# A graph attention layer in split fp32: the first turned tile's high part and the first half slab's low part change engines

## The chip, the cores and the metric

The kernel runs on one core of one Trainium2 chip. The metric is device time in microseconds (us) of that core, in runs without a profiler; three runs of the kernel before gave 288.67, 288.79 and 288.88 us. The median is 288.79 us.

## What is computed

The reference is one graph attention layer on 384 nodes with 1024 features (N = 384, F = 1024, 16 heads of 64). Cut to what matters:

```python
h = relu(layernorm(x))                       # 384 x 1024
q, k, v = h @ wq.T + bq, h @ wk.T + bk, h @ wv.T + bv
q2, k2, v2 = q @ wiq.T + biq, k @ wik.T + bik, v @ wiv.T + biv
scores = q2 . k2 * 0.125 + mask              # per head, mask from 6528 edges
out = softmax(scores) @ v2                   # per head
return x + out @ wo.T + bo
```

## The kernel before, in words

**Split products.** Every fp32 factor of a matrix product is kept as a high part (the value rounded to the matmul's fp32r form, names ending in `_hi`) and a low part (value minus high part, `_lo`). A product is then three matmuls into one PSUM bank: high by high, weight-low by high, high by feature-low. TensorE's time is almost all such triples, over 56 weight slabs of 128 x 1024 that stream in from memory through three buffers `raw` and are split into four pairs `w_hi`, `w_lo`.

**Who does what.** The order on each engine is written out by hand, one program per engine, and semaphores join them. ScalarE makes the high parts of the slabs, VectorE the low parts of slabs 2 to 52, GpSimd those of slabs 0, 1 and the last ones. SyncE issues slab `s` when slab `s - 3` has its low part (for slab 3 also when `half_lo` is there, line 376).

**The start**, where the change is. The rows of `x` come in three tiles of 128 rows (t = 0, 1, 2).
- VectorE takes each tile's statistics, GpSimd the reciprocal root (`rstd`, line 447), ScalarE scales tiles 0 and 1 (line 591). For the last tile VectorE subtracts and clips (line 806), and the scaling is shared: ScalarE scales columns 0 to 511 in two pieces (line 581), VectorE columns 512 to 1023 (line 810, semaphore `h_last_ok`).
- TensorE turns h so that features lie on partitions: 24 transposes of 128 x 128 (`turn_h`, line 1032), eight for each tile. For the last tile the order of k is 0, then 4 to 7 (after `h_last_ok`), then 1, 2, 3. The eight turned tiles `k` of 128 x 384 stand in PSUM; `h_turned` counts them as they are complete.
- ScalarE splits the first half of slab 0 (line 577, `half_hi`) before its share of the last scaling. Then it copies the eight turned tiles to `a_hi` (line 603, `h_hi`): tile 0 as soon as one is turned, tile 1 when six are turned, that is when k = 1 is, tile 2 when seven are, the rest when all are.
- VectorE, after line 810, makes the low part of the first half of slab 0 (line 812, `half_lo`), the high part of the second half (line 815, `early_hi`), and then the eight low parts `a_lo` of the turned tiles (line 856, `h_lo`), each after its `a_hi`.
- GpSimd, after the last `rstd` (line 447), makes the low part of slab 0's second half (line 470, `slab_lo`), then both halves of slab 1 (lines 455 and 458).
- TensorE's `first_tile` follows the turns: per `k` it multiplies slab 0's high part (line 1072) and low part (line 1075) with `a_hi[k]`, and, two steps behind, slab 0's high part with `a_lo[k]` (line 1062, `low_part`). It waits for `half_hi`, for each `a_hi`, for `half_lo` before the first low product, for `slab_lo` before `k` = 4, and for each `a_lo`. Its 24 matmuls are followed without a gap by the tiles of lines 983 to 985.

Of the kernel before, what the change touches and what calls it, by code (L numbers as in the profile page):

```python
# [12 lines left out]
F32 = mybir.dt.float32  # L13
# [4 lines left out]
ALU = mybir.AluOpType  # L18
# [8 lines left out]
KT = F // P  # L27
# [8 lines left out]
HALF = 512  # L36
# [41 lines left out]
def gat_kernel(nc, slabs, x, edge_cols, edge_rows, edge_weights, biases, bo, out):  # L78
    with ExitStack() as ctx:
        def sb(name, shape, dt):  # L80
            return ctx.enter_context(nc.sbuf_tensor(name, shape, dt))

        def sem(name):
            return ctx.enter_context(nc.semaphore(name))
# [3 lines left out]
        a_hi = sb("a_hi", [P, KT, N], F32R)  # L88
# [6 lines left out]
        raw = sb("raw", [P, RAW, F], F32)  # L95
        w_hi = sb("w_hi", [P, RING, F], F32R)
        w_lo = sb("w_lo", [P, RING, F], F32R)
# [68 lines left out]
        def cell_rows(c):  # L166
# [30 lines left out]
        mask_step, mask_ok = sem("mask_step"), sem("mask_ok")  # L197
        stats_step, stats_agg, eps_ok, rstd_ok, shift_ok, h_ok = (
            sem("stats_step"), sem("stats_agg"), sem("eps_ok"), sem("rstd_ok"), sem("shift_ok"), sem("h_ok"))
        h_step, h_last_ok = sem("h_step"), sem("h_last_ok")  # L200
        h_turned, h_hi, h_lo = sem("h_turned"), sem("h_hi"), sem("h_lo")
        half_hi, half_lo, early_hi, second_lo = sem("half_hi"), sem("half_lo"), sem("early_hi"), sem("second_lo")
        second_hi = sem("second_hi")
# [17 lines left out]
        def h_all(k):  # L221

            return h_bank[k][:, 0:N] if k < KT - 1 else banks[:, 0:NT, N:N + P]

        def as_turned(a, k):

            return a[:, k, :] if k < KT - 1 else a[:, k, :].rearrange("p (t m) -> p t m", m=P)
# [32 lines left out]
        def tile_place(t):  # L260

            if t < KT:
                return b_hi[:, t, :], b_lo[:, t, :], bias[:, BV + t:BV + t + 1], tile_bank[t % 2]
            if t < 3 * KT:
                j = t - KT
                hi, lo = (b_hi, b_lo) if j < KT else (c_hi, c_lo)
                return hi[:, j % KT, :], lo[:, j % KT, :], bias_qk[:, j // 2, j % 2:j % 2 + 1], tile_bank[t % 2]
            pair, x = (t - 3 * KT) // 2, t % 2
            hi, lo, b = [(q2_hi, q2_lo, BIQ), (k2_hi, k2_lo, BIK)][x]
            return hi[:, :], lo[:, :], bias[:, b + pair:b + pair + 1], bank[pair_place(pair) + x]  # L270
# [28 lines left out]
        def split_place(s):  # L299

            j = s - O0 - KS
            if Q0 <= s < QK0:
                first = (s - s % 2) % RING
                return tuple(a[:, first:first + 2, :].rearrange("p a (k x d) -> p a k x d", x=2, d=D)[:, :, :, s % 2, :]
                             for a in (w_hi, w_lo))
            if j < 0:
                return w_hi[:, s % RING, :], w_lo[:, s % RING, :]
            hi, lo = (b_hi, b_lo) if j < 3 else (c_hi, c_lo)
            part = slice(j % 3 * F, (j % 3 + 1) * F)
            return tuple(a[:, :, :].rearrange("p k n -> p (k n)")[:, part] for a in (hi, lo))  # L310
# [24 lines left out]
        def wait_lo(eng, s):  # L335

            eng.wait_ge(slab_lo_dve if lo_by_vector(s) else slab_lo, lo_count(s))
# [24 lines left out]
        def _(sp_eng):  # L362
# [50 lines left out]
            for i, (_, n, cols_out, _) in enumerate(out_pieces):  # L413
                sp_eng.wait_ge(out_ok, i + 1)
                sp_eng.dma_start(out[n * P:(n + 1) * P, cols_out], y[:, n, cols_out]).then_inc(stored, 16)
# [3 lines left out]
        def _(pool):  # L419
# [44 lines left out]
            def pair_lo_part(pair):  # L464
                pool.wait_ge(head_hi, pair + 1)
                nc.gpsimd.tensor_tensor(a_lo[:, pair, :], head_out, a_hi[:, pair, :].bitcast(F32),
                                        ALU.subtract).then_inc(head_lo, 1)

            pool.wait_ge(early_hi, 1)
            nc.gpsimd.tensor_tensor(w_lo[:, 0, HALF:F], raw[:, 0, HALF:F], w_hi[:, 0, HALF:F].bitcast(F32),  # L470
                                    ALU.subtract).then_inc(slab_lo, 1)
# [66 lines left out]
        def _(act):  # L538
# [6 lines left out]
            def tile_hi_part(t):  # L545
                hi, _, b, psum = tile_place(t)
                act.wait_ge(slab_used, slabs_done(t))
                if t == KT:
                    act.wait_ge(bias_ok, 4)
                nc.scalar.activation(hi, psum[:, 0:N], ACT.Identity, bias=b).then_inc(tile_hi, 1)  # L550
# [28 lines left out]
            def scale_last(part):  # L579

                nc.scalar.activation(x_sb[:, NT - 1, part], x_sb[:, NT - 1, part], ACT.Copy,
                                     scale=rstd[:, NT - 1:NT]).then_inc(h_ok, 1)
# [3 lines left out]
            for t in range(NT):  # L586
# [6 lines left out]
                else:  # L593
                    act.wait_ge(h_step, 1)
                    act.wait_ge(rstd_ok, NT)
                    for part in (slice(0, P), slice(P, HALF)):
                        scale_last(part)
            for k in range(KT):
                if k == KT - 1:
                    act.wait_ge(h_lo, NT)  # L600

                act.wait_ge(h_turned, 1 if k == 0 else min(k + 1 + KT // 2, KT))
                nc.scalar.activation(as_turned(a_hi, k), h_all(k), ACT.Copy).then_inc(h_hi, 1)
                if k == KT - 3:
                    act.wait_ge(slab_in[1], 16)
                    nc.scalar.activation(w_hi[:, 1, 0:HALF], raw[:, 1, 0:HALF], ACT.Copy).then_inc(second_hi, 1)
# [109 lines left out]
        def _(dve):  # L716
# [87 lines left out]
            for b in range(2):  # L804
# [3 lines left out]
            dve.wait_ge(rstd_ok, NT)  # L808
            dve.wait_ge(h_step, 2)
            nc.vector.tensor_scalar(h_last, h_last, rstd[:, NT - 1:NT], None, ALU.mult).then_inc(h_last_ok, 1)  # L810
            dve.wait_ge(half_hi, 1)
            nc.vector.tensor_tensor(w_lo[:, 0, 0:HALF], raw[:, 0, 0:HALF], w_hi[:, 0, 0:HALF].bitcast(F32),
                                    ALU.subtract).then_inc(half_lo, 1)
            dve.wait_ge(slab_in[0], 16)
            nc.vector.tensor_copy(w_hi[:, 0, HALF:F], raw[:, 0, HALF:F]).then_inc(early_hi, 1)

# [35 lines left out]
                                               op1=ALU.add).then_inc(mask_ok, 1)  # L852

            for k in range(KT):
                dve.wait_ge(h_hi, k + 1)
                nc.vector.tensor_tensor(as_turned(a_lo, k), h_all(k), as_turned(a_hi, k).bitcast(F32),
                                        ALU.subtract).then_inc(h_lo, 1)
            edge_sign()
# [116 lines left out]
            for i, (_, n, cols_out, psum) in enumerate(out_pieces):  # L975
                dve.wait_ge(out_done, i + 1)
                nc.vector.tensor_tensor(y[:, n, cols_out], psum, y[:, n, cols_out], ALU.add).then_inc(out_ok, 1)

        @block.tensor
        def _(pe):  # L980
# [73 lines left out]
            def first_tile():  # L1054

                hi, lo = split_place(0)
                psum = tile_place(0)[3]

                def low_part(k):

                    pe.wait_ge(h_lo, k + 1)
                    return nc.tensor.matmul(psum[:, 0:N], hi[:, k * P:(k + 1) * P], a_lo[:, k, :], start=False,  # L1062
                                            stop=(k == KT - 1))


                pe.wait_ge(half_hi, 1)
                for k in range(KT):
                    c = slice(k * P, (k + 1) * P)
                    pe.wait_ge(h_hi, k + 1)
                    if k == KT // 2:  # L1070
                        wait_lo(pe, 0)
                    nc.tensor.matmul(psum[:, 0:N], hi[:, c], a_hi[:, k, :], start=(k == 0), stop=False)  # L1072
                    if k == 0:
                        pe.wait_ge(half_lo, 1)
                    nc.tensor.matmul(psum[:, 0:N], lo[:, c], a_hi[:, k, :], start=False, stop=False)  # L1075
                    if k >= 2:
                        low_part(k - 2)
                low_part(KT - 2)
                low_part(KT - 1).then_inc(slab_used, 1)

            first_tile()
            for t in range(KT):
                if t >= 1:
# [218 lines left out]
```

## Time and profile before

| What | Value |
| --- | --- |
| median of three runs | 288.79 us |
| profiled execution, its own time | 289.49 us |
| span of its profile | 287.7 us |
| busy: TensorE, VectorE, ScalarE, GpSimd | 281.7, 177.8, 158.0, 151.6 us |
| granted TensorE clock, mean | 1.0 |

The span runs from the first to the last instruction in the profile; the execution's own time has 1.8 us around it. The profiled execution took 0.70 us more than the median run. A busy time is the sum over an engine's instructions, and says nothing of what waited for what.

### The profile page before, as it was taken

The page shows a single profiled execution, that of the slowest core. Times are in us where ns is not written, and L with a number is a line of the kernel's source. Part 1 is how long each engine was busy: PE and PEld are TensorE (multiplying, and loading weights), DVE is VectorE, ACT ScalarE, POOL GpSimd, SP SyncE. Part 2 cuts the span into 40 slices and gives each one's busy share as a digit, 9 for nine tenths or more (in the row PEclk, how much of TensorE's full clock was granted, in tenths as well). Part 3 has the DMA queues.
Part 4 walks back from the last instruction along what each step waited for, and adds up shares of the span by engine and source line. Part 5 has one row for each costly group of instructions (what it writes and reads, how often), then busy time and mean ns, then how long its engine had stood idle before and what let it go on. Part 6 is the DMA issues. An engine that isn't in the chain of part 4 may idle for free.

```text
span 287.7 us, 6029 instructions
## 1 busy us (share of the span) xinstructions
PE 281.7 (98%) x2361; PEld 266.1 (92%) x2361; DVE 177.8 (62%) x442; ACT 158.0 (55%) x287; POOL 151.6 (53%) x157
## 2 busy tenths in 40 slices
PE   6999999999999999999999999999999999999996
PEld 3899998888899999999999999999999999898885
DVE  4999878777588443335564877666667566754221
ACT  2986444193166434323442697977878787985000
POOL 6451354545345765545102597957658494786100
PEclk9999999999999999999999999999999999999999
DMA  7978955744942334455947323605132231221032
GB/s 261 317 246 267 343 202 170 237 154 134 366 159 79 126 96 143 146 146 119 266 117 179 75 66 84 148 8 142 47 102 75 73 90 62 76 99 49 0 146 75
DMA packets 16080, 40.92 MB, mean 142 GB/s; under 512 B 3738, under 2 KB 5171, under 8 KB 16051
## 3 DMA queue, kind: packets, MB, share of 16 engines
q1 hardware_dynamic: 13602, 38.53, 42.7%
q0 software_dynamic: 2016, 1.21, 1.8%
q10 hardware_dynamic: 432, 0.79, 0.7%
q8 instruction: 19, 0.31, 0.4%
q14 instruction: 11, 0.08, 0.1%
HBM read 37.71 MB, written 2.81 MB: 141 GB/s over the span
## 4 chain that ended last, share of the span: by engine, by line
PE 95%; DVE 2%; issue 1%; ACT 1%; POOL 0%; POOLq 0%; ACTq 0%
PE banks L1110 24%; PE banks L983 17%; PE banks L985 17%; PE banks L984 17%; PE banks L1176 6%; PE banks L1129 4%; PE banks L1158 3%; PE banks L1208 3%; PE banks L1028 2%; DVE v L830 1%; PE banks L1032 1%; PE banks L1072 1%; ACT v L570 1%; PE banks L1075 0%; PE banks L1062 0%
## 5 line engine op out<-in xcount | busy, mean ns | idle before, releaser
L489 POOL DMA_INDIRECT cells<-value,cell x51 | 54.1, 1061 | 53.7 <-DMA cells<-value,cell 37.9
L543 ACT ACTIVATE w_hi<-raw 128x1024 fp32r<-128x1024 f32 x50 | 51.8, 1055 | 23.2 <-PE banks L985 19.1
L983 PE MATMUL banks<-a_hi,w_hi 128*128 128x384 f32 x184 | 61.5, 334 | 0.7 <-DVE b_lo L820 0.7
L985 PE MATMUL banks<-a_lo,w_hi 128*128 128x384 f32 x184 | 61.5, 334 | 0.0
L984 PE MATMUL banks<-a_hi,w_lo 128*128 128x384 f32 x184 | 61.5, 334 | 0.0
L462 POOL TENSOR_TENSOR w_lo<-raw,w_hi 128x1024 fp32r<-128x1024 f32 x15 | 36.7, 2451 | 41.0 <-ACT w_hi L543 41.0
L843 DVE TENSOR_TENSOR w_lo<-raw,w_hi 128x1024 fp32r<-128x1024 f32 x35 | 42.3, 1228 | 10.7 <-ACT w_hi L543 10.7
L983 PEld LDWEIGHTS banks<-a_hi,w_hi 128*128 128x128 f32 x184 | 34.5, 188 | 1.0 <-issue 1.0
L984 PEld LDWEIGHTS banks<-a_hi,w_lo 128*128 128x128 f32 x184 | 34.5, 188 | 0.0
L985 PEld LDWEIGHTS banks<-a_lo,w_hi 128*128 128x128 f32 x184 | 34.5, 188 | 0.0
L655 ACT ACTIVATE prob<-prob,neg_max 128x384 f32<-128x384 f32 x48 | 29.0, 605 | 5.2 <-DVE neg_max L903 5.2
L515 POOL TENSOR_SCALAR prob<-prob,row_inv 128x384 f32<-128x384 f32 x48 | 28.2, 604 | 4.0 <-DVE row_inv L911 3.9
L903 DVE CUSTOM_DVE_ANT_0 prob<-banks,work 128x384 f32<-128x384 f32 x48 | 24.7, 555 | 8.9 <-PE banks L1129 8.6
L917 DVE TENSOR_TENSOR pt_lo<-banks,pt_hi 128x768 fp32r<-128x768 f32 x24 | 21.7, 952 | 9.4 <-ACT pt_hi L666 9.4
L1110 PE MATMUL banks<-b_hi,w_hi 64*128 64x384 f32 x128 | 23.9, 347 | 0.0
L1110 PE MATMUL banks<-c_hi,w_lo 64*128 64x384 f32 x128 | 23.0, 331 | 0.0
L1110 PE MATMUL banks<-c_lo,w_hi 64*128 64x384 f32 x128 | 23.0, 331 | 0.0
L1110 PE MATMUL banks<-c_hi,w_hi 64*128 64x384 f32 x128 | 23.0, 331 | 0.0
L1110 PE MATMUL banks<-b_lo,w_hi 64*128 64x384 f32 x128 | 23.0, 332 | 0.0
L1110 PE MATMUL banks<-b_hi,w_lo 64*128 64x384 f32 x128 | 22.9, 332 | 0.0
L666 ACT ACTIVATE pt_hi<-banks 128x768 fp32r<-128x768 f32 x24 | 17.9, 810 | 2.1 <-PE banks L1158 2.0
L985 PE MATMUL banks<-w_lo,b_hi 128*128 128x512 f32 x48 | 18.7, 389 | 0.0
(152 smaller groups left out, 590.2 us busy)
## 6 DMA issues: line engine op xcount, KB each, us to landing
raw<-in_slabs SPq DMA_DIRECT2D x40, 512.0 KB
raw<-in_slabs SPq DMA_DIRECT2D x32, 256.0 KB
prob<-key_rows SPq DMA_DIRECT2D x8, 256.0 KB, 3.7
x_sb<-in_x SPq DMA_DIRECT2D x3, 512.0 KB
out_y<-x_sb SPq DMA_DIRECT2D x5, 256.0 KB, 2.1
cells<-prob SPq DMA_DIRECT2D x2, 576.0 KB, 8.0
cells<-value,cell POOLq DMA_INDIRECT x51
x_sb<-in_x ACTq DMA_DIRECT2D x3, 256.0 KB, 4.6
```

Source lines behind the costliest of these rows:

```text
L462: nc.gpsimd.tensor_tensor(lo, raw[:, s % RAW, :], hi.bitcast(F32), ALU.subtract).then_inc(slab_lo, 1)
L489: nc.gpsimd.indirect_dma_start(out=cells[c][:, :], out_offset=bass.IndirectOffsetOnAxis(ap=cell[:, t:t + 1], axis=0), in_=value[:, t:t + 1 ...
L515: nc.gpsimd.tensor_scalar(prob_chunk(j, n, x), prob_chunk(j, n, x), row_inv[:, j % 2, c:c + 1], 1.0, ALU.mult, ALU.mult).then_inc(prob_ok, 1)
L543: nc.scalar.activation(split_place(s)[0], raw_place(s), ACT.Copy).then_inc(slab_hi, 1)
L655: nc.scalar.activation(prob_chunk(j, n, x), prob_chunk(j, n, x), ACT.Exp, scale=-1.0, bias=neg_max[:, j % 2, c:c + 1], accum_out=row_sum[: ...
L843: nc.vector.tensor_tensor(lo, raw_place(s), hi.bitcast(F32), ALU.subtract).then_inc(slab_lo_dve, 1)
L903: nc.vector.tensor_tensor_reduce(out=prob_chunk(j, n, x), in0=in_blocks(bank[score_place(n) + x][:, 0:N]), in1=in_blocks(mask[:, n, :]), s ...
L917: nc.vector.tensor_tensor(as_turned_probs(pt_lo, m), turned(pair, m), as_turned_probs(pt_hi, m).bitcast(F32), ALU.subtract).then_inc(pt_lo ...
L983: nc.tensor.matmul(psum, w[0], a[0], start=first, stop=False)
L984: nc.tensor.matmul(psum, w[1], a[0], start=False, stop=False)
L985: return nc.tensor.matmul(psum, w[0], a[1], start=False, stop=last)
L1110: mm = nc.tensor.matmul(bank[pair_place(pair) + x][:, 0:N], w[own, k * P:(k + 1) * P], a[own, block_at % KT, :], start=(step == 0), stop=( ...
```

## The change

VectorE now copies turned tile 0 to `a_hi` (new semaphore `h_first`), at the place where it made the first half slab's low part. GpSimd makes that low part, ahead of its other half slab. ScalarE copies tiles 1 to 7 only. Whoever waited for `h_hi` waits for `h_first` at k = 0 and for a count that is one lower after it. Nothing is added or left out of the computation.

```diff
@@ gpsimd, after the last rstd
+            pool.wait_ge(half_hi, 1)
+            nc.gpsimd.tensor_tensor(w_lo[:, 0, 0:HALF], raw[:, 0, 0:HALF], w_hi[:, 0, 0:HALF].bitcast(F32),
+                                    ALU.subtract).then_inc(half_lo, 1)
             pool.wait_ge(early_hi, 1)
@@ scalar
-            for k in range(KT):
+            for k in range(1, KT):
                 if k == KT - 1:
                     act.wait_ge(h_lo, NT)

-                act.wait_ge(h_turned, 1 if k == 0 else min(k + 1 + KT // 2, KT))
+                act.wait_ge(h_turned, min(k + 1 + KT // 2, KT))
                 nc.scalar.activation(as_turned(a_hi, k), h_all(k), ACT.Copy).then_inc(h_hi, 1)
@@ vector, after line 810
-            dve.wait_ge(half_hi, 1)
-            nc.vector.tensor_tensor(w_lo[:, 0, 0:HALF], raw[:, 0, 0:HALF], w_hi[:, 0, 0:HALF].bitcast(F32),
-                                    ALU.subtract).then_inc(half_lo, 1)
+            dve.wait_ge(h_turned, 1)
+            nc.vector.tensor_copy(as_turned(a_hi, 0), h_all(0)).then_inc(h_first, 1)
@@ vector (the low parts) and tensor (first_tile), the same edit in both
-                dve.wait_ge(h_hi, k + 1)
+                if k == 0:
+                    dve.wait_ge(h_first, 1)
+                else:
+                    dve.wait_ge(h_hi, k)
```

VectorE's order from the scaling of the last tile to the low parts, before (`h_last` is a part of `x_sb`):

```order
L810 TENSOR_SCALAR x_sb<-x_sb,rstd 128x512 [waits h_step,rstd_ok]
L812 TENSOR_TENSOR w_lo<-raw,w_hi 128x512 [waits half_hi]
L815 CAST w_hi<-raw 128x512 [waits slab_in0]
L856 TENSOR_TENSOR a_lo<-banks,a_hi 128x384 [waits h_hi] x8
```

and in the changed kernel, whose lines lie a few further down (813 is 810, 817 is 815, 861 is 856):

```order
L813 TENSOR_SCALAR x_sb<-x_sb,rstd 128x512 [waits h_step,rstd_ok]
L815 CAST a_hi<-banks 128x384 [waits h_turned]
L817 CAST w_hi<-raw 128x512 [waits slab_in0]
L861 TENSOR_TENSOR a_lo<-banks,a_hi 128x384 [waits h_first]
L861 TENSOR_TENSOR a_lo<-banks,a_hi 128x384 [waits h_hi] x7
```

The subtraction over 512 columns is gone, and a copy of 384 columns out of PSUM, which waits for the first turned tile, stands in its place.

GpSimd's order from the last `rstd` on, before:

```order
L447 TENSOR_TENSOR rstd<-mean_var,minus_half 128x1 [waits stats_agg]
L470 TENSOR_TENSOR w_lo<-raw,w_hi 128x512 [waits early_hi]
L455 TENSOR_TENSOR w_lo<-raw,w_hi 128x512 [waits second_hi]
```

and in the changed kernel:

```order
L447 TENSOR_TENSOR rstd<-mean_var,minus_half 128x1 [waits stats_agg]
L470 TENSOR_TENSOR w_lo<-raw,w_hi 128x512 [waits half_hi]
L473 TENSOR_TENSOR w_lo<-raw,w_hi 128x512 [waits early_hi]
L455 TENSOR_TENSOR w_lo<-raw,w_hi 128x512 [waits second_hi]
```

A third half-slab subtraction stands ahead of the two others, right behind the last `rstd`; line 470 is now the first half, line 473 the second.

## Rows read from the trace of the kernel before

**Rows 1.** Page: the chain that ended last, by engine.
```profile
PE 95%; DVE 2%; issue 1%; ACT 1%; POOL 0%; POOLq 0%; ACTq 0%
```
**Rows 2.** Waits of TensorE (engine line waited for: us, times, longest).
```profile
PE banks L983 <- DVE b_lo L820: 0.7, 1, 0.7
```
**Rows 3.** Timeline of TensorE, 10.6 to 12.2 (start us, us, engine, line, operation, count).
```profile
10.60 0.33 PE L1032 MATMUL banks<-ident,x_sb 128*128 128x128 f32 x1
...
11.20 0.38 PE L1032 MATMUL banks<-ident,x_sb 128*128 128x128 f32 x2
...
11.60 0.41 PE L1072 MATMUL banks<-a_hi,w_hi 128*128 128x384 f32 x1
...
12.06 0.44 PE L1072 MATMUL banks<-a_hi,w_hi 128*128 128x384 f32 x1
```
**Rows 4.** Timeline of ScalarE, 9.4 to 12.0.
```profile
9.43 0.62 ACT L577 ACTIVATE w_hi<-raw 128x512 fp32r<-128x512 f32 x1
...
10.97 0.49 ACT L603 ACTIVATE a_hi<-banks 128x384 fp32r<-128x384 f32 x1
...
11.51 0.49 ACT L603 ACTIVATE a_hi<-banks 128x384 fp32r<-128x384 f32 x1
```
**Rows 5.** Timeline of VectorE, 10.1 to 15.5.
```profile
10.12 0.49 DVE L810 TENSOR_SCALAR x_sb<-x_sb,rstd 128x512 f32<-128x512 f32 x1
10.52 0.68 DVE L812 TENSOR_TENSOR w_lo<-raw,w_hi 128x512 fp32r<-128x512 f32 x1
11.12 0.42 DVE L815 CAST w_hi<-raw 128x512 fp32r<-128x512 f32 x1
11.49 3.99 DVE L856 TENSOR_TENSOR a_lo<-banks,a_hi 128x384 fp32r<-128x384 f32 x8
...
12.04 1.95 DVE L856 TENSOR_TENSOR a_lo<-banks,a_hi 128x384 fp32r<-128x384 f32 x4
```
**Rows 6.** Timeline of GpSimd, 9.2 to 12.9.
```profile
9.18 0.87 POOL L447 TENSOR_TENSOR rstd<-mean_var,minus_half 128x1 f32<-128x1 f32 x1 [0.91 <-DVE mean_var L801]
...
11.62 1.30 POOL L470 TENSOR_TENSOR w_lo<-raw,w_hi 128x512 fp32r<-128x512 f32 x1 [1.57 <-DVE w_hi L815]
```
**Rows 7.** Timelines of VectorE and GpSimd, 15.4 to 16.8.
```profile
15.40 0.16 DVE L735 TENSOR_SCALAR sp<-ew 128x4 f32<-128x4 f32 x1
15.41 1.30 POOL L458 TENSOR_TENSOR w_lo<-raw,w_hi 128x512 fp32r<-128x512 f32 x1
15.47 1.26 DVE L736 TENSOR_SCALAR sp<-ew 128x4 f32<-128x4 f32 x1
```
**Rows 8.** Timelines of both at 166, and line 462 (ns min/median/max).
```profile
166.02 1.22 DVE L933 TENSOR_TENSOR x_sb<-x_sb,prob 128x1024 f32<-128x1024 f32 x1
166.43 3.08 POOL L462 TENSOR_TENSOR w_lo<-raw,w_hi 128x1024 fp32r<-128x1024 f32 x1 [0.39 <-ACT w_hi L543]
...
L462 POOL TENSOR_TENSOR w_lo<-raw,w_hi x15: 2396/2402/3081, 156.2 to 252.5; 128x1024 fp32r<-128x1024 f32 x15
```
**Rows 9.** TensorE's weight loads (PEld) in the first tile, and its end.
```profile
11.68 0.19 PEld L1075 LDWEIGHTS banks<-a_hi,w_lo 128*128 128x128 f32 x1
...
13.42 0.19 PEld L1072 LDWEIGHTS banks<-a_hi,w_hi 128*128 128x128 f32 x1
...
15.68 0.19 PEld L1062 LDWEIGHTS banks<-a_lo,w_hi 128*128 128x128 f32 x1
...
16.03 0.33 PE L983 MATMUL banks<-a_hi,w_hi 128*128 128x384 f32 x1
```
**Rows 10.** Downstream: slab 3, the second tile's low part, TensorE's fourth tile; DMA share.
```profile
17.74 1.06 ACT L543 ACTIVATE w_hi<-raw 128x1024 fp32r<-128x1024 f32 x1 [0.22 <-DMA raw<-in_slabs]
...
23.14 0.62 DVE L820 SCALAR_TENSOR_TENSOR b_lo<-banks,bias,b_hi 128x384 fp32r<-128x384 f32 x1
...
24.35 0.33 PE L983 MATMUL banks<-a_hi,w_hi 128*128 128x384 f32 x1
...
14.00:15.00 1.00, 1.00 (x8) 0.99 (x7) 0.99 (x3) 1.00 (x4) 0.87 (x1) 1.00 1.08 406
```

More of the change, by code:

```diff
@@ L199, in gat_kernel @@
             sem("stats_step"), sem("stats_agg"), sem("eps_ok"), sem("rstd_ok"), sem("shift_ok"), sem("h_ok"))
-        h_step, h_last_ok = sem("h_step"), sem("h_last_ok")
+        h_step, h_last_ok, h_first = sem("h_step"), sem("h_last_ok"), sem("h_first")
         h_turned, h_hi, h_lo = sem("h_turned"), sem("h_hi"), sem("h_lo")
@@ L1068, in first_tile @@
                     c = slice(k * P, (k + 1) * P)
-                    pe.wait_ge(h_hi, k + 1)
+                    if k == 0:
+                        pe.wait_ge(h_first, 1)
+                    else:
+                        pe.wait_ge(h_hi, k)
                     if k == KT // 2:
```

## The prediction

> **What bounds the kernel now.** I read the chain that ended last first: TensorE is 95% of it [rows 1], and its list of waits has one entry behind the start, 0.7 us at about 86 us for a low part of VectorE [rows 2]. From the end of the first tile on, TensorE runs almost without a gap, so the change is worth exactly what it does to the moment when TensorE leaves its first tile, 16.03 us [rows 9], unless something further down absorbs or enlarges that. What matters is the stretch from 10.1 to 16.0 us, read engine by engine.
>
> TensorE first [rows 3]. The first transpose of the last tile starts at 10.60, the one of k = 1 at 11.20 (a row of two, 0.11 apart, so its result stands at about 11.48), and the first product of the first tile at 11.60. The next high product comes at 12.06 only; at full pace it would have come two matmuls of 0.17, or 0.35, after the first. That is the hole that one might hope to close. ScalarE explains it [rows 4]: `a_hi[0]` is made from 10.97 to 11.46, `a_hi[1]` from 11.51 to 12.00, and TensorE goes on at 12.06.
>
> But what held `a_hi[1]`? ScalarE starts back-to-back copies 0.1 before the last one ends, which would be 11.36. It started at 11.51, 0.03 after the transpose of k = 1 was done, and by the program it waits for just that (six tiles turned). So ScalarE was waiting for TensorE, not for its own copy of tile 0. **Taking that copy off ScalarE frees 0.37 us of an engine that then waits for the same transpose.** `a_hi[1]` and all behind it stay where they are, if the transposes do.
>
> **The change part by part.**
>
> *ScalarE* loses 0.49 us of work and gains nothing that can be passed on. Zero.
>
> *GpSimd's new half slab.* It needs `half_hi`, which ends at 9.43 + 0.62 = 10.05 [rows 4], and GpSimd itself is free at 9.18 + 0.87 = 10.05 [rows 6]. GpSimd starts 0.08 after another engine's result (line 470 at 11.62, after the cast that ends at 11.54 [rows 5, 6]), so at 10.13. VectorE starts line 810 at 10.12 [rows 5]: the two start within 0.01 us of each other. This matters since they can hold each other up. A VectorE operation on four columns took 1.26 us where its twin took 0.16, and ended at 16.73, right behind the GpSimd subtraction that ran from 15.41 to 16.71 [rows 7]. The other way round, a GpSimd subtraction that started at 166.43, inside a VectorE one, took 3.08 us against a median of 2.40, and ended 2.27 after the VectorE one had (169.51 less 167.24) [rows 8]. Which is held? Whoever starts first goes on; and the twin of 0.16 us started 0.01 *before* GpSimd and was not held, while the one that started 0.06 after was. At 10.12 VectorE is again 0.01 ahead. My forecast is that VectorE goes first.
>
> Then line 810 ends at 10.61 as now, and so do the transposes. GpSimd, held until 10.61, needs the rest: of 2.40 us for 1024 columns and 1.30 for 512 [rows 6, 8], 1.10 go to 512 columns; behind a release 1024 columns took 2.27, so 512 take 1.17. `half_lo` is ready at **11.78**; before it was 10.52 + 0.68 = 11.20 [rows 5]. TensorE loads these weights at 11.68 now [rows 9]; that moves to 11.83 (a load follows its data by 0.05), 0.15 late. The hole before 12.06 has the room: the six products of k = 0, 1, 2 need 1.04 at full pace. About 0.
>
> *VectorE's copy of tile 0.* The first tile is turned at 10.60 + 0.33 = 10.93, so the copy starts at about 10.98. No row shows a VectorE copy out of PSUM. Nearest below is the cast of 512 columns inside SBUF, 0.42; nearest above the subtraction of 384 columns with one operand in PSUM, 0.55 (the row of four spans 1.95, starting every 0.47) [rows 5]. I take 0.55, for the same PSUM operand and width; `a_hi[0]` is then ready at 11.53, not 11.46, and the first product moves by 0.07 at most, or with 0.42 forward by what the last transposes allow, 0.07. Both vanish in the hole before 12.06. The Trainium skill ("VectorE: DVE Perf Modes", on PSUM operands) says that fp32 out of PSUM runs at one column a cycle; by its cost table (120 + 384 cycles at 0.96 GHz, 0.525 us, an estimate) the sum would be 0.02 less.
>
> *The cast that follows* (`early_hi`) would start at 11.45 where it started at 11.12, but GpSimd is at work until 11.78. A cast inside SBUF is of the kind that I count as held: it ends some 0.28 behind the release, at **12.06** against 11.54 now. So the eight low parts begin at 12.01 instead of 11.49. They start every 0.47 us, their source is there in time, and the last ends at 12.01 + 7 x 0.465 + 0.55 = **15.82**, against 15.48 now (two waits for `a_hi` that they had on the way take up 0.2). TensorE loads the weights of its last low product at 15.68 [rows 9], before that is there: the load moves to 15.87, by 0.19. As the load runs 0.17 ahead of its product, part may be made good; between 0.02 and 0.19 I take **+0.10**.
>
> *Slab 0's second half* on GpSimd starts at 12.14 and ends at 13.44, where it ended at 12.92 [rows 6]. TensorE's load for k = 4 stands at 13.42 [rows 9]: 0.07 late, from 0 to 0.07, inside the same delay and not added to it.
>
> *Downstream.* SyncE issues slab 3 with that low part, 0.5 later. Its data stood behind the fill of the mask cells in a saturated queue (DMA share 1.08 from 14 to 15 us), and ScalarE took slab 3 at 17.74. What follows on VectorE ends with the second tile's low part, 23.14 + 0.62 = 23.76, which TensorE needs at 24.35: 0.4 to 0.5 of room [rows 10]. I expect 0 to 0.3 of lateness there and cost it at nothing; with all 0.5 it would be 0.1.
>
> The sum is +0.10 against the profiled execution's 289.49. That one lies 0.70 above the median, but nothing in the sum is proportional to it, so I add it to the median: 288.79 + 0.10 = **288.9 us**. A measurement of this kernel tells 0.2%, or 0.58 us, from no change.
>
> **The rivals.**
>
> *GpSimd first (slower).* If GpSimd has begun when VectorE wants line 810, that line ends about 0.33 behind GpSimd's 10.13 + 1.30 = 11.43, at 11.76, not 10.61. It gives `h_last_ok`, for which the transposes of k = 4 to 7 wait, and those of 1, 2, 3 stand behind them on TensorE: k = 1 moves by 1.15, with it `a_hi[1]` and the whole tile, and nothing is queued elsewhere that makes it good. 288.79 + 1.15 = 289.94 us. It decides at a lead of GpSimd somewhere between 0 and 0.06 us [rows 7], which is a matter of one or two hundredths here. For it speaks how near the tie is; against it that the twin was not held at a lead of 0.01. The Trainium skill ("SBUF — State Buffer", on who interferes with whom) has this as a rule: the two engines share a pair of SBUF ports, the first to start holds it for its whole instruction, and the other blocks fully. By that rule, the traces agree both ways round. Chance 0.17.
>
> *The copy out of PSUM is held as well.* It would wait for 11.78 and end near 12.2; the cast and the low parts follow, the last ending near 16.3, and the tile ends about 0.6 late: 289.4 us. Against it: the low parts of line 856, which read PSUM and one SBUF operand, start every 0.47 and keep that pace beside GpSimd's work from 11.62 to 12.92 [rows 5, 6]. Chance 0.06.
>
> *ScalarE was the brake after all (faster).* If the freed copy brings `a_hi[1]` forward, at most the holes between 11.53 and 12.90 close, some 0.33 us: 288.5 us, which would not be told from no change. Chance 0.05.
>
> *Something further down moves.* The wait of 0.7 us at 86 us [rows 2] could shrink or grow as the transfers before it shift: 288.1 to 289.5. Chance 0.04.
>
> **How the numbers follow.** The forecast has 0.68, between 288.7 and 289.1. With the rivals, faster by over 0.2% needs the last one on its good side: 0.04. Slower by over 0.2%: GpSimd first 0.17, half of the held copy 0.03, the last one's bad side 0.02, so 0.22. Same: 0.74. The range goes from 288.4, for the closing holes, to 290.1, to hold the tie that falls the other way.
>
> **What would show it.** Line 813 near 10.12 with 0.49 us, and GpSimd's line 470 with 1.65 instead of 1.30: VectorE went first. Line 813 with 1.6 us and line 470 with 1.30: it was the rival. The copy (815) near 10.98 with 0.42 to 0.56. The cast (817) stretched to about 0.6. ScalarE's first copy still at 11.51. The first matmul of line 983's group near 16.1. I am wrong in the mechanism if ScalarE's first copy starts before 11.4, or if no operation of either engine is stretched.

## The result

The changed kernel takes **290.18 us** (median of ten runs), the kernel before 288.82 us in the same comparison: a ratio of 1.005, interval 1.004 to 1.006. That is 1.2 to 1.7 us more. I had forecast 288.9 us and no change that can be told; what happened is the rival "GpSimd first", for which I had worked out 289.94 us and given 0.17. My range ended at 290.1 us. In the experiments below two runs were far longer than the others of their kernel (990.55 us with GpSimd in two pieces, 296.23 us with one empty instruction); the ratios leave them out, the medians as recorded do not, and without them these two medians are 289.44 and 288.8 us.

The profiled execution took 290.15 us, its span is 288.4 us. Its chain is led by TensorE less than before [rows 1], with VectorE's scaling of the last tile (line 813) among its lines:

```profile
PE 89%; DMA 5%; DVE 3%; ACT 1%; issue 0%; SPq 0%; DVEq 0%; ACTq 0%
PE banks L1118 24%; PE banks L988 16%; PE banks L989 16%; PE banks L990 16%; PE banks L1184 6%; PE banks L1137 4%; PE banks L1166 3%; PE banks L1216 3%; DMA raw<-in_slabs 2%; DMA x_sb<-in_x 2%; DVE v L832 1%; ACT w_hi L546 1%; PE banks L1080 1%; DVE x_sb L813 1%; ACT v L573 1%; PE banks L1067 0%
```

The waits of TensorE have a new entry, 0.8 us for line 813, and another of 0.5 us for ScalarE's scaling of the second tile: in this execution VectorE waited 0.5 us for the rows of the last tile (at 7.72), in that of before it did not. The entry that answers to [rows 2] is shorter:

```profile
PE banks L1037 <- DVE x_sb L813: 0.8, 1, 0.8
PE banks L1037 <- ACT x_sb L594: 0.5, 1, 0.5
PE banks L988 <- DVE b_lo L822: 0.2, 1, 0.2
```

The timeline of VectorE in the changed kernel (answers to [rows 5]):

```profile
10.35 1.55 DVE L813 TENSOR_SCALAR x_sb<-x_sb,rstd 128x512 f32<-128x512 f32 x1
11.82 0.54 DVE L815 CAST a_hi<-banks 128x384 fp32r<-128x384 f32 x1
12.29 0.41 DVE L817 CAST w_hi<-raw 128x512 fp32r<-128x512 f32 x1
```

and that of GpSimd (answers to [rows 6]):

```profile
9.41 0.87 POOL L447 TENSOR_TENSOR rstd<-mean_var,minus_half 128x1 f32<-128x1 f32 x1 [0.68 <-DVE mean_var L804]
10.35 1.27 POOL L470 TENSOR_TENSOR w_lo<-raw,w_hi 128x512 fp32r<-128x512 f32 x1
```

Both start at 10.35, as near as I had worked out. But the scaling takes 1.55 us instead of 0.49, and ends at 11.90, 0.28 behind GpSimd's subtraction (11.62), which takes its plain time. What waits for the scaling shows on TensorE and ScalarE (answers to [rows 3, 4, 9]):

```profile
11.96 0.33 PE L1037 MATMUL banks<-ident,x_sb 128*128 128x128 f32 x1 [0.80 <-DVE x_sb L813]
...
12.70 0.42 PE L1080 MATMUL banks<-a_hi,w_hi 128*128 128x384 f32 x1
12.96 0.33 PE L1083 MATMUL banks<-a_hi,w_lo 128*128 128x384 f32 x1
13.30 0.44 PE L1080 MATMUL banks<-a_hi,w_hi 128*128 128x384 f32 x1
...
17.29 0.33 PE L988 MATMUL banks<-a_hi,w_hi 128*128 128x384 f32 x1
```

```profile
12.76 0.87 ACT L606 ACTIVATE a_hi<-banks 128x384 fp32r<-128x384 f32 x2 [1.48 <-PE banks L1037]
```

The transposes go on at 11.96, ScalarE's first copy starts at 12.76 behind them, after 1.48 us of idle time, and the second tile's first matmul (line 988, 983 before) comes at 17.29 instead of 16.03.

The profiled executions differ by up to 0.5 us in when the last `rstd` ends (9.98 to 10.47), since the rows of `x` arrive at different times, so I compare from a point that lies behind that: **from the end of the last `rstd` to the second tile's first matmul** it is 16.03 - 10.05 = 5.98 us before, and 17.29 - 10.28 = 7.01 us now. The first tile costs 1.03 us. This length, called the stretch below, is read in the same way from the one profiled execution of every kernel.

### The profile page after: what moved, and what is told of

Read it like the earlier page. It is cut to its first block, busy times and chain, and to the rows that moved or that the text cites. A ratio compares the mean times of both kernels' runs of the same rounds, so it can differ in the third digit from the quotient of the medians.

```text
span 288.4 us, 6029 instructions
## 1 busy us (share of the span) xinstructions
PE 281.7 (98%) x2361; PEld 265.6 (92%) x2361; DVE 178.8 (62%) x442; ACT 157.3 (55%) x286; POOL 153.3 (53%) x158
## 4 chain that ended last, share of the span: by engine, by line
PE 89%; DMA 5%; DVE 3%; ACT 1%; issue 0%; SPq 0%; DVEq 0%; ACTq 0%
PE banks L1118 24%; PE banks L988 16%; PE banks L989 16%; PE banks L990 16%; PE banks L1184 6%; PE banks L1137 4%; PE banks L1166 3%; PE banks L1216 3%; DMA raw<-in_slabs 2%; DMA x_sb<-in_x 2%; DVE v L832 1%; ACT w_hi L546 1%; PE banks L1080 1%; DVE x_sb L813 1%; ACT v L573 1%; PE banks L1067 0%
```

## The experiments

Theory A is the rival's: GpSimd's subtraction, once under way, holds VectorE's scaling, and through `h_last_ok` the transposes. Theory B says that the moved copy costs. All were compared with the kernel before on the same chip, whose median was 288.83 us beside the first four, 288.73 beside the next four and 288.71 beside the last three. The intervals are of the ratio to it. The number of runs per kernel lies between 4 (two waits more) and 12.

| Run | stretch, us | median, us | ratio (interval) |
| --- | --- | --- | --- |
| before | 5.98 | 288.8 | |
| the change | 7.01 | 290.18 | 1.005 (1.004 to 1.006) |
| GpSimd's part alone | 6.99 | 289.90 | 1.0034 (1.0022 to 1.0047) |
| the copy alone | 6.06 | 289.15 | 1.0006 (0.9995 to 1.0017) |
| VectorE's scaling first | 6.25 | 289.21 | 1.0016 (1.0004 to 1.0028) |
| scaling cut 511 + 1 | 7.15 | 290.20 | 1.0049 (1.0031 to 1.0068) |
| GpSimd in two pieces | 6.49 | 289.61 | 1.0031 (1.0018 to 1.0044) |
| scaling with a running sum | 6.23 | 289.06 | 1.0005 (0.9996 to 1.0015) |
| one wait more | 7.05 | 289.76 | 1.0033 (1.0022 to 1.0043) |
| two waits more | 7.04 | 290.05 | 1.0042 (1.0027 to 1.0057) |
| one empty instruction | 6.03 | 288.83 | 1.0006 (0.9997 to 1.0016) |
| two empty instructions | 6.03 | 288.87 | 1.0003 (0.9994 to 1.0012) |
| tile 4 second (from before) | 5.98 | 288.57 | 0.9997 (0.9988 to 1.0006) |

**GpSimd's part alone.** The copy is back on ScalarE, VectorE has neither job (of the edit to the changed kernel only VectorE's lines are shown; ScalarE's loop and the waits are those of before).

```diff
-            dve.wait_ge(h_turned, 1)
-            nc.vector.tensor_copy(as_turned(a_hi, 0), h_all(0)).then_inc(h_first, 1)
```

> Only GpSimd's part of the change: it makes the first half slab's low part, the copy of tile 0 stays on ScalarE, and VectorE has neither. Theory A: the scaling of the last tile is stretched to about 1.55 us as in the changed kernel, k = 1 is turned 1.0 to 1.15 us late, total 289.9 to 290.3 us. Theory B: 288.8 us as before.

Measured 289.90 us. VectorE's scaling in its timeline:

```profile
10.30 1.55 DVE L813 TENSOR_SCALAR x_sb<-x_sb,rstd 128x512 f32<-128x512 f32 x1
```

The stretch is 6.99 us: the whole loss comes with GpSimd's part, none of it needs the copy. Theory B falls.

**The copy alone.** GpSimd is as before, VectorE keeps its subtraction and copies tile 0 behind it (shown against the kernel before, VectorE's lines only).

```diff
             dve.wait_ge(half_hi, 1)
             nc.vector.tensor_tensor(w_lo[:, 0, 0:HALF], ...).then_inc(half_lo, 1)
+            dve.wait_ge(h_turned, 1)
+            nc.vector.tensor_copy(as_turned(a_hi, 0), h_all(0)).then_inc(h_first, 1)
```

> Only the copy of tile 0 is moved to VectorE, behind the half slab's low part, which stays there. Theory A: the scaling takes 0.49 us, the copy 0.54 us, ScalarE's first copy still starts at the transpose of k = 1, that is where its second one started before; the low parts end 0.3 us later and the tile 0 to 0.2 us: 288.9 us (288.8 to 289.1). Theory B: 290 us or more.

Measured 289.15 us, not told from before by its interval; the stretch is 0.08 longer. ScalarE's first copy starts 1.46 us after the last `rstd` ended (11.94 and 10.47), as its second one did before (11.51 and 10.05). So freeing ScalarE brought nothing forward.

**VectorE's scaling first.**

```diff
+            pool.wait_ge(h_last_ok, 1)
             pool.wait_ge(half_hi, 1)
             nc.gpsimd.tensor_tensor(w_lo[:, 0, 0:HALF], ...)
```

> The changed kernel, but GpSimd takes up the first half slab's low part only after VectorE has scaled the last tile (it waits for h_last_ok). Theory A (GpSimd's subtraction, once begun, holds VectorE's scaling of the last tile and with it the transposes): the scaling is back at 0.49 us and starts and ends first, GpSimd's subtraction follows it from 0.08 behind its end and takes 1.3 us, the cast of early_hi is held until that ends; the tile ends 0.3 us late, total 289.1 us (288.9 to 289.3). Theory B (the copy of tile 0 on VectorE is what costs): nothing comes back, 290.1 to 290.4 us.

Measured 289.21 us. The timelines of VectorE and GpSimd in this run:

```profile
10.27 0.49 DVE L814 TENSOR_SCALAR x_sb<-x_sb,rstd 128x512 f32<-128x512 f32 x1
...
11.12 0.56 DVE L816 CAST a_hi<-banks 128x384 fp32r<-128x384 f32 x1 [0.36 <-PE banks L1038]
11.60 0.80 DVE L818 CAST w_hi<-raw 128x512 fp32r<-128x512 f32 x1
```

```profile
10.84 1.28 POOL L471 TENSOR_TENSOR w_lo<-raw,w_hi 128x512 fp32r<-128x512 f32 x1 [0.64 <-DVE x_sb L814]
```

With nothing but the order at this place changed, 0.76 us of the stretch come back. The copy out of PSUM runs beside GpSimd in 0.56 us; the cast inside SBUF behind it is held until GpSimd is through at 12.12, and takes 0.80. What is left, 0.27, comes in two waits of TensorE:

```profile
12.17 0.19 PEld L1084 LDWEIGHTS banks<-a_hi,w_lo 128*128 128x128 f32 x1 [0.19 <-POOL w_lo L471]
```

```profile
12.48 1.30 POOL L474 TENSOR_TENSOR w_lo<-raw,w_hi 128x512 fp32r<-128x512 f32 x1 [0.36 <-DVE w_hi L818]
```

The first low product waits for the half slab that GpSimd now makes later; behind that TensorE is 0.12 late. The held cast makes slab 0's second half late as well (it ends at 13.78), the load of weights for k = 4 comes 0.12 behind that, at 13.90, and behind it TensorE is 0.26 late. The low parts `a_lo` add 0.01.

**The scaling cut in 511 and 1 columns**, to take it out of the mode in which it handles two columns a cycle.

```diff
-            nc.vector.tensor_scalar(h_last, h_last, rstd[:, NT - 1:NT], None, ALU.mult).then_inc(h_last_ok, 1)
+            for part in (slice(HALF, F - 1), slice(F - 1, F)):
+                piece = x_sb[:, NT - 1, part]
+                nc.vector.tensor_scalar(piece, piece, rstd[:, NT - 1:NT], None, ALU.mult).then_inc(h_last_ok, 1)
```

TensorE waits for both pieces (that line is not shown).

> The changed kernel with VectorE's scaling of 512 columns cut into 511 and 1, odd counts in both. Theory A in its narrow form (only an operation that works at two columns a cycle needs what GpSimd holds): both pieces run beside GpSimd's subtraction, the long one in about 0.69 us instead of 1.56, h_last_ok is 0.27 us late, total 289.1 us (289.0 to 289.4). If any VectorE operation from SBUF to SBUF is held: 290.2 us or more, the pieces ending behind GpSimd's.

Measured 290.20 us.

```profile
10.38 1.55 DVE L815 TENSOR_SCALAR x_sb<-x_sb,rstd 128x511 f32<-128x511 f32 x1
```

It is held, and ends 0.28 behind GpSimd's 11.65, as 512 columns do. The form of the next experiment takes 0.25 us more than the plain one takes unhindered (0.74 and 0.49 us for 512 columns), and no such addition shows behind the release. So I take it that an odd count did not change the mode, and the run tells nothing of what a slower mode would do. That is what the Trainium skill says too ("VectorE: DVE Perf Modes", the mode table: even counts, or equal ones for source and destination); I had overlooked the second half.

**The scaling with a running sum as a second output.** The extra column of sums is read by nothing.

```diff
-            nc.vector.tensor_scalar(h_last, h_last, rstd[:, NT - 1:NT], None, ALU.mult).then_inc(h_last_ok, 1)
+            nc.vector.tensor_scalar(h_last, h_last, rstd[:, NT - 1:NT], 0.0, ALU.mult, ALU.add,
+                                    accum_out=shift[:, NT - 1:NT]).then_inc(h_last_ok, 1)
```

> The changed kernel with VectorE's scaling written with a running sum as a second output (into a column of shift that nothing reads); the sum is not part of the computation. The Trainium skill (SBUF — State Buffer, who interferes with whom) says that this form does not work on two columns a cycle and so does not contend. If so, theory A in its narrow form expects it to run beside GpSimd's subtraction in 0.7 to 0.8 us instead of 1.56, h_last_ok 0.2 to 0.35 us later than before, from the last rstd to the second tile's first matmul 6.2 to 6.4 us, total 289.2 us (289.0 to 289.5). If any VectorE operation from SBUF to SBUF is held by GpSimd's reads: 7.0 us or more, total 290.1 us or more.

Measured 289.06 us, which is not told from before. VectorE and GpSimd in this run:

```profile
10.35 0.74 DVE L813 TENSOR_SCALAR_CACHE_REDUCE x_sb<-x_sb,rstd 128x512 f32<-128x512 f32 x1
```

```profile
10.33 1.27 POOL L470 TENSOR_TENSOR w_lo<-raw,w_hi 128x512 fp32r<-128x512 f32 x1
```

GpSimd started first, by 0.02 us, and nobody was held: VectorE's form ended 0.5 us before GpSimd did, and GpSimd took its plain 1.27. So it is not VectorE as such that GpSimd holds, but this form of its work. The Trainium skill's page "SBUF — State Buffer" (who interferes with whom) names exactly this exception, and the trace agrees.

**GpSimd's subtraction in two pieces** of 256 columns.

```diff
-            nc.gpsimd.tensor_tensor(w_lo[:, 0, 0:HALF], ...).then_inc(half_lo, 1)
+            for part in (slice(0, HALF // 2), slice(HALF // 2, HALF)):
+                nc.gpsimd.tensor_tensor(w_lo[:, 0, part], ...).then_inc(half_lo, 1)
```

(Arguments cut; whoever waits for `half_lo` waits for both pieces.)

> The changed kernel with GpSimd's new subtraction in two instructions of 256 columns. Theory A (VectorE is held for one instruction of GpSimd): the first piece takes about 0.75 us, VectorE's scaling gets in between the two and ends some 0.5 us earlier than in the changed kernel, the second piece waits for it; from the last rstd to the second tile's first matmul 6.4 to 6.6 us (before 5.98, changed 7.01), total 289.4 us (289.2 to 289.8). Theory C (VectorE waits until GpSimd has nothing more ready, since GpSimd takes up its next instruction before the last one ends): the scaling ends later than now, 7.1 us or more, total 290.2 us or more.

Measured 289.61 us.

```profile
10.33 1.01 DVE L814 TENSOR_SCALAR x_sb<-x_sb,rstd 128x512 f32<-128x512 f32 x1
```

```profile
10.33 1.59 POOL L471 TENSOR_TENSOR w_lo<-raw,w_hi 128x256 fp32r<-128x256 f32 x2
```

VectorE got in between the two, ended at 11.34 instead of 11.90, and the second piece waited for it. The hold of VectorE lasts for one instruction of GpSimd; half an instruction, half the loss (the stretch is 0.51 longer than before, not 1.03).

**How much lead does VectorE need?** Four runs delay GpSimd's start by a little. First by more waits, on semaphores that have long come:

```diff
             pool.wait_ge(half_hi, 1)
+            pool.wait_ge(h_step, 2)
```

> The changed kernel with one more wait ahead of GpSimd's new subtraction, on a semaphore that has long come (h_step), which costs GpSimd the handling of one wait, 0.05 to 0.08 us. Theory A with a tie that GpSimd won by less than that: VectorE is now first, the scaling takes 0.49 us, GpSimd's subtraction is stretched to 1.6 us, from the last rstd to the second tile's first matmul 6.05 to 6.25 us, total 288.9 to 289.2 us. If GpSimd claims what they share well before its start in the profile, or is served first whoever comes first: nothing changes, 7.0 us, 290.0 to 290.3 us.

> As the run with one more wait, with two (also stats_agg, long there too): VectorE leads by 0.1 us or more. Theory A: 288.9 to 289.2 us, as with one wait, or, if one was too little, only here. If GpSimd is served first whoever comes first within 0.1 us: 7.0 us, 290.0 to 290.3 us.

Measured 289.76 and 290.05 us. With one wait more:

```profile
10.26 1.59 DVE L814 TENSOR_SCALAR x_sb<-x_sb,rstd 128x512 f32<-128x512 f32 x1
```

```profile
10.30 1.27 POOL L471 TENSOR_TENSOR w_lo<-raw,w_hi 128x512 fp32r<-128x512 f32 x1
```

VectorE leads by 0.04 us and is still held. The second wait added no delay (a lead of 0.03, again held); why not is not shown. Then by an instruction that does nothing:

```diff
             pool.wait_ge(half_hi, 1)
+            nc.gpsimd.engine_nop().then_inc(lead, 1)
+            pool.wait_ge(lead, 1)
```

> The changed kernel with one empty instruction of GpSimd between its wait for half_hi and the new subtraction, passed on by a semaphore of its own: it begins 0.05 to 0.1 us later, so VectorE leads by that. With 0.04 us of lead VectorE lost. If GpSimd's claim counts from within 0.1 us of its start: VectorE is now first, its scaling takes 0.49 us, GpSimd's subtraction 1.6 to 1.7 us; the forecast of the prediction is then tried as it was meant: from the last rstd to the second tile's first matmul 6.05 to 6.25 us (before 5.98, changed 7.01), total 288.9 to 289.1 us. If GpSimd is served first whatever the lead: 7.0 us and 290.0 us.

> The same with two empty instructions, a lead of 0.1 to 0.2 us. If the lead decides, VectorE is first here even if it was not with one: 6.05 to 6.3 us, total 288.9 to 289.2 us. If GpSimd is served first whenever it asks before VectorE is through: 7.0 us or more and 290.0 us.

Measured 288.83 and 288.87 us. The run with one empty instruction:

```profile
10.09 0.49 DVE L816 TENSOR_SCALAR x_sb<-x_sb,rstd 128x512 f32<-128x512 f32 x1
10.94 0.56 DVE L818 CAST a_hi<-banks 128x384 fp32r<-128x384 f32 x1 [0.36 <-PE banks L1040]
11.41 0.58 DVE L820 CAST w_hi<-raw 128x512 fp32r<-128x512 f32 x1
```

```profile
10.16 1.55 POOL L473 TENSOR_TENSOR w_lo<-raw,w_hi 128x512 fp32r<-128x512 f32 x1
```

```profile
16.05 0.34 PE L991 MATMUL banks<-a_hi,w_hi 128*128 128x384 f32 x1
```

A lead of 0.07 us turns it round: the scaling takes 0.49, GpSimd is the one that is held (1.55 instead of 1.27), and the kernel is not told from before. With two empty instructions the lead is 0.14 and the result the same. An instruction that does nothing, ahead of the moved one, takes back the whole loss of the change.

**Tile 4 second.** From the kernel before: is there anything to win in the hole before tile 1?

```diff
+TILE_ORDER = [0, 4, 1, 2, 3, 5, 6, 7]
-            for k in range(KT):
+            for i, k in enumerate(TILE_ORDER):
-                act.wait_ge(h_turned, 1 if k == 0 else min(k + 1 + KT // 2, KT))
+                act.wait_ge(h_turned, (1, 2, 6, 7)[i] if i < 4 else KT)
```

VectorE's low parts and TensorE's products follow the same order, tile 4's high product second (those edits are not shown).

> The kernel before with another order in the first tile: tile 4, turned second, is copied to a_hi second and multiplied second, in the hole in which TensorE waits for tile 1. GpSimd and VectorE keep their work. This asks what closing the hole is worth at most: from the last rstd to the second tile's first matmul 5.80 to 5.90 us instead of 5.98, total 288.5 to 288.8 us, hardly to be told from before (288.8). If the hole is set by something else than the transpose of k = 1: 5.98 us or more.

Measured 288.57 us, not told from before, and a stretch of 5.98: no gain. ScalarE's copies follow each other without a pause; the second to the fourth (tiles 4, 1 and 2):

```profile
11.39 1.25 ACT L607 ACTIVATE a_hi<-banks 128x384 fp32r<-128x384 f32 x3
```

Tile 4's product filled the hole at 12.06, but the copy of tile 1 started at 11.76 instead of 11.51 and ended at 12.25, and its high product came at 12.30. TensorE gained nothing: its eighth product starts at 13.11, 1.48 behind its first, and before it was 13.07, 1.47 behind. The pause of ScalarE that I had found, 0.15 us, was too short for a whole copy; they follow each other every 0.37.

## Why the prediction was wrong

**The step that failed** is the order of the two engines: "the twin of 0.16 us started 0.01 *before* GpSimd and was not held ... At 10.12 VectorE is again 0.01 ahead. My forecast is that VectorE goes first." GpSimd went first, VectorE's scaling took 1.55 us instead of 0.49, and the stretch grew by 1.03. The tie was there, but I read the order of starts wrongly. The twin stood at 15.40 [rows 7], and line 458 of GpSimd followed on line 455 without a pause there: its row begins at 15.41, while line 455, from 14.13 for 1.30 us, was still at work until 15.42. I take it that in such a row GpSimd's own work begins later than the row does, so that the twin was further ahead than 0.01; no run tests this. At 10.12 both engines came out of a wait, and there VectorE's start has to lie further ahead: 0.00, 0.03 and 0.04 us were too little, 0.07 and 0.14 enough. So it is VectorE that needs a lead, between 0.04 and 0.07 us, and not GpSimd, for which I had put 0 to 0.06. No row of before has two such starts, and nothing in the rows spoke for a chance as small as 0.17. By the Trainium skill's rule on the port pair ("SBUF — State Buffer", who interferes with whom) the one that starts first holds it; by the starts that the profile shows, VectorE was 0.04 ahead in one run and lost, so here the measurement decides: the rule does not resolve starts this close.

The other steps, with the run of one empty instruction as the kernel that I had forecast (it is another kernel, and shows what would have followed had VectorE gone first; the forecast of the changed kernel stays wrong):
- *ScalarE's freed time brings nothing.* Right. Where it leaves out tile 0 and VectorE's scaling takes its 0.49 us, its first copy starts 1.46 to 1.47 behind the last `rstd`, as its second one did before; in the changed kernel it comes behind the late transposes.
- *GpSimd held: 1.17 behind the release, `half_lo` at 11.78.* Measured 11.71 less 10.58, 1.14. Right.
- *The copy of tile 0: 0.55, not held beside GpSimd.* Measured 0.56 beside GpSimd, 0.54 in the changed kernel, where GpSimd was through. Right, and the rival that it is held falls.
- *The cast stretched to about 0.6, ending 0.28 behind the release.* Measured 0.58, and 0.28. Right.
- *The tile 0.10 late, 288.9 us.* Measured 0.05, and 288.83 us. The size is near, the place isn't the one I had priced, the last low product. Its load is 0.12 later than before, counted from the last `rstd` (5.75 and 5.63), but the product behind it loses nothing that shows; with two empty instructions it loses 0.02. Of the 0.05, 0.03 appear at k = 4, where TensorE waits for slab 0's second half (through at 13.38 in this run), which I had counted inside the other delay. So it was luck in part that the sum came out.

```profile
13.49 0.19 PEld L1083 LDWEIGHTS banks<-a_hi,w_hi 128*128 128x128 f32 x1
...
15.77 0.19 PEld L1070 LDWEIGHTS banks<-a_lo,w_hi 128*128 128x128 f32 x1
```

- *The rival's price of 1.15.* The stretch is 1.03 longer: the scaling ended 0.28 behind GpSimd, not 0.33, and GpSimd took 1.27, not 1.30. The median rose by 1.36, 0.3 more than the stretch.

**What stays open** is that 0.3. Runs with the same stretch differ as much: 289.76 and 290.05 us with more waits, 289.90 with GpSimd's part alone. A place where the start's lateness can grow or be absorbed is the wait near 87 us [rows 2]: TensorE waits there for a low part of VectorE (line 822), and the chain goes back from it over VectorE and ScalarE to a slab's transfer. In the changed kernel that transfer is the longest piece of the chain between 70 and 90 us:

```profile
73.53 7.11 DMA raw<-in_slabs
...
87.00 0.63 DVE b_lo L822
```

The wait was 0.7 us in the profiled execution of before, 0.2 in the changed one, 0.3 with two waits more, and under 0.1 in the ten others. It accounts for most of what the profiled executions differ by behind the first tile: from the second tile's first matmul to the end of the span they need 270.8 to 271.6 us (before 271.6, the changed kernel 271.1), and with this wait taken off 270.8 to 271.0 (270.9 to 271.0 for both kernels). So in the profiled executions nothing behind the first tile but this wait tells the two kernels apart. Ahead of the stretch the last `rstd` ends at 10.05 before and at 10.28 in the changed kernel. How the late rows and this wait are spread over the runs without a profile isn't shown, so neither is it shown that they account for the 0.3.

## What to carry to other kernels

When work moves to GpSimd, look on VectorE for scalings and casts from SBUF to SBUF that overlap it: each can wait for the whole GpSimd instruction, as the scaling did here, and what hangs on the VectorE one matters, not what GpSimd's result is needed for. Where two such starts come out within a tenth of a microsecond, don't bet on one of them: put an order between them, or use pieces or a form that isn't held. Before freeing an engine, ask what its next instruction waits for; here it waited for another engine, and the freed time was worth nothing.

## What the runs showed of the hardware

- Two starts that look simultaneous are decided within 0.07 us: VectorE's scaling lost to GpSimd's subtraction with a lead of 0.04 us (1.59 us instead of 0.49) and won with 0.07.
- VectorE is held for one instruction of GpSimd (two pieces halved the loss, 0.51 instead of 1.03 us) and ends 0.28 us behind it with 512 columns. The other way round GpSimd's 512 columns end 1.14 us behind VectorE's instruction.
- A scaling of 511 columns in place is held like one of 512: 1.55 us, ending 0.28 behind GpSimd.
- The same scaling with a running sum takes 0.74 us beside GpSimd, is not held, and holds nobody (GpSimd 1.27 us); here it is the better form (289.06 us against 290.18), although the plain one takes 0.49 where nothing holds it. A copy of 384 columns out of PSUM isn't held either (0.56 us).
- A satisfied wait on a semaphore, put ahead of a GpSimd instruction that waits for another, delayed its start by 0.03 to 0.04 us; an empty instruction with its own semaphore delayed it by about 0.07, two by 0.14 (one profiled execution each).
